# First sequence's triangular substitution issued on VectorE instead of GpSimd, in a four-stage transformer kernel

## The reference, cut to what matters

```python
att = jnp.where(tri, 0.0, -(kb @ jnp.swapaxes(k, -1, -2)))
for i in range(1, chunk):                      # chunk = 32
    upd = jnp.einsum('bhnj,bhnjk->bhnk', att[..., i, :], att)
    att = att.at[..., i, :i].add(upd[..., :i])
att = att + jnp.eye(chunk)
u = att @ v
w = att @ kb
```

## Time and profile before

| | us |
|---|---|
| three runs | 1975.06, 1981.21, 1982.22 |
| their median | 1981.21 |
| the profiled execution, device time | 1968.41 |
| its span, first to last instruction | 1966.6 |
| PE busy in the span | 1678.3 (85%) |
| DVE busy | 992.2 (50%) |
| POOL busy | 760.8 (39%) |
| ACT busy | 545.7 (28%) |

### The profile page before, as it was taken

One profiled execution on the slowest core, in us unless ns is written; L12 is line 12 of the kernel. 1 busy time (PEld: TensorE's weight loads), 2 busy tenths in 40 slices (PEclk: granted clock), 3 DMA queues, 4 the chain that ended last, 5 costly groups with the idle time before them and its releaser, 6 DMA issues. The chain is left out here.

```text
span 1966.6 us, 22843 instructions
## 1 busy us (share of the span) xinstructions
PE 1678.3 (85%) x8588; PEld 1121.4 (57%) x8588; DVE 992.2 (50%) x2206; ACT 545.7 (28%) x1180; POOL 760.8 (39%) x948
## 2 busy tenths in 40 slices
PE   4368898998999898896279999999967999999997
PEld 2245656666665666574236766666654555565564
DVE  3438798989898988784711111101113333444422
ACT  3242525253534435222221111111102222222121
POOL 1656667675757575812034423333221110111100
PEclk9679899898989999878589999999988999999999
DMA  3010111111111111101323322333120000000000
GB/s 106 17 22 17 23 49 23 44 27 28 44 28 44 28 34 28 33 12 32 129 86 86 86 47 56 81 79 82 22 50 4 3 20 22 22 22 22 11 0 22
DMA packets 108318, 77.99 MB, mean 40 GB/s; under 512 B 57384, under 2 KB 101424, under 8 KB 108208
## 3 DMA queue, kind: packets, MB, share of 16 engines
q1 hardware_dynamic: 95920, 59.74, 10.6%
q0 software_dynamic: 12288, 16.79, 4.9%
HBM read 51.34 MB, written 25.17 MB: 39 GB/s over the span
## 5 line engine op out<-in xcount | busy, mean ns | idle before, releaser
L383 DVE SCALAR_TENSOR_TENSOR a_firT<-a_v_ch,a_fir_lw,a_firT 128x511 f32<-128x511 f32 (+14 forms) x480 | 341.8, 777 | 0.0
L1530 DVE TENSOR_SCALAR ex_y<-ps,gT 128x256 f32<-128x256 f32 x64 | 31.0, 484 | 409.1 <-PE ps L1485 409.1
L1485 PE MATMUL ps<-ex_w,ex_hT 128*128 128x256 f32 x1024 | 223.5, 379 | 0.0
L1474 PE MATMUL ps<-ex_xT,ex_w 128*128 128x512 f32 x512 | 222.1, 594 | 0.0
L1440 POOL DMA_INDIRECT acc_dram<-ex_y,idxT x64 | 100.0, 1563 | 293.8 <-DVE ex_y L1530 293.8
L1485 PEld LDWEIGHTS ps<-ex_w,ex_hT 128*128 128x128 f32 x1024 | 194.0, 190 | 29.5 <-issue 3.8
L1512 ACT ACTIVATE ex_hT<-ps 128x512 f32<-128x512 f32 x128 | 76.6, 598 | 368.1 <-PE ps L1474 368.1
L1474 PEld LDWEIGHTS ps<-ex_xT,ex_w 128*128 128x128 f32 x512 | 97.7, 191 | 119.6 <-issue 119.2
L693 POOL TENSOR_TENSOR a_prod<-a_Yp,a_spare 128x126 f32<-128x126 f32 (+22 forms) x248 | 152.9, 616 | 26.4 <-DMA a_Yp<-y_dram 6.9
L1087 PE MATMUL ps<-a_firT,a_w_f 128*128 128x512 f32 x256 | 133.2, 645 | 18.7 <-DVE a_firT L383 18.7
L695 POOL TENSOR_TENSOR a_spare<-a_spare,a_prod 128x126 f32<-128x126 f32 (+22 forms) x248 | 133.0, 536 | 19.4
(11 more groups left out here) (275 smaller groups left out, 2947.1 us busy)
## 6 DMA issues: line engine op xcount, KB each, us to landing
ex_w<-in_L_ffn_w SPq DMA_DIRECT2D x16, 1024.0 KB, 8.6
a_xa<-in_L_attn_hidden_states SPq DMA_DIRECT2D x8, 512.0 KB, 4.0
a_xr<-in_L_attn_hidden_states SPq DMA_DIRECT2D x8, 512.0 KB, 4.6
a_Yp<-y_dram SPq DMA_DIRECT2D x16, 256.0 KB, 3.7
acc_dram<-a_xr SPq DMA_DIRECT2D x8, 512.0 KB, 4.3
xn_dram<-a_gxn SPq DMA_DIRECT2D x8, 512.0 KB, 3.2
l_xw<-acc_dram SPq DMA_DIRECT2D x8, 512.0 KB, 3.9
out<-l_xw SPq DMA_DIRECT2D x8, 512.0 KB, 2.9
```

What stands on the lines that cost most here:

```text
L383: nc.vector.scalar_tensor_tensor(out[:, kind, c, s:], v, w[:, c, n - 1 - s:n - s], out[:, kind, c, s:], ALU.mult, ALU.add).then_inc(fir_st ...
L1474: ins = nc.tensor.matmul(ps[:, n % 4, :], w1[j][:, c, f * P:(f + 1) * P], xT[j][:, c, half * 512:(half + 1) * 512], start=c == 0, stop=c = ...
L1485: ins = nc.tensor.matmul(dn_slot(n), hT[half][:, f, (n % 4) * CAP:(n % 4 + 1) * CAP], w2[j][:, f, :], start=f == 0, stop=f == FB - 1)
```

## The change

The substitution of sequence 0 is issued by DVE, between `norm_rows` of sequence 1 and the 20 early taps. POOL still clears and seeds `spare` for that sequence, and then goes straight on to `vk_of`. The other seven sequences stay on POOL. The products, the additions, their shapes and the semaphore counts are the same.

```diff
+            def solve_first():
+
+                dve.wait_ge(Yp_in, 32)
+                for k in range(31):
+                    c, r = k // 2 + 1, 31 - k
+                    m = prod[:, 0:c * r].rearrange("p (c i) -> p c i", c=c)
+                    dve.wait_ge(solved, 3 + 2 * k)
+                    nc.vector.tensor_tensor(m, spread(Yp[:, k + 1:32, k], 1, c), spread(Tp[:, 0:c, k], 2, r), ALU.mult).then_inc(solved, 1)
+                    dve.wait_ge(solved, 4 + 2 * k)
+                    nc.vector.tensor_tensor(Tp[:, 0:c, k + 1:32], Tp[:, 0:c, k + 1:32], m, ALU.add).then_inc(solved, 1)
+
             def join(b, d, e, r):
...
                 if nxt is not None:
                     norm_rows(nxt)
+                if b == 0:
+                    solve_first()
                 if d is not None:
                     scan(d, 3)
                 more(FIR_EARLY)
...
                 for half in range(2):
                     pool.memset(spare[64 * half:64 * half + 64, half:512:34], 1.0).then_inc(solved, 1)
+                if b == 0:
+                    pool.wait_ge(solved, n + 3)
+                    return
                 pool.wait_ge(Yp_in, b * 32 + 32)
```

## The result

The changed kernel takes 1956.39 us (median of four runs, 1951.79 to 1959.66) against 1978.35 us for the kernel before in the same comparison, a ratio of 0.9887 with a 95% interval of 0.9854 to 0.992. That is some 22 us less, with 16 to 29 us inside the interval. Run again with more repetitions the ratio is 0.9897 (0.9874 to 0.9921), or 20 us. The forecast was 19.1 us, 1962.1 us, within 1948 to 1972.

A forecast was written before the change was run, and what follows sets the result against it. POOL's 38.1 us substitution of sequence 0 was taken to hold up the first merge; on DVE it ends at 88.5 (69.52 + 17.7 + 1.3) instead of 107.61, 19.1 us off the 1981.21 us median: 1962.1 us, range 1948 to 1972.

The forecast's parts named there:

- The hole and what ends it: Before the first merge: PE, DVE and ACT empty from 83.8 to 107.6 us, ended by POOL's substitution, store and load.
- What is removed: On POOL: 62 substitution instructions leave, with 28.1 us after the first product and the stall; `vk` starts 41 us earlier.
- the 9.88 us: First product of POOL's substitution of sequence 0: its length, read as POOL kept from its operands by DVE's taps.
- that rival: At POOL's first `vk` product: the stall is POOL's own and moves there; gain 11.1 us, 1970.1 us, chance 0.06.
- The price on DVE: Substitution on DVE: 17.7 us for 62 instructions plus 1.3 us for meeting POOL's `vk`, ending at 88.5.
- POOL's `vk`: Beside the start of DVE's substitution: four of eight products each block a DVE instruction, up to 0.33 us, 1.3 us.
- Strided reads: Products reading a column of `Yp` on DVE: elements cost double, 2.9 us more; gain 16.2, 1965.0 us, chance 0.10.
- the row I judged it by: DVE instruction reading one element of four, 16 bytes apart: 0.17 us for 16 elements, as dense, so no penalty shows.
- the fit from two pairs: DVE instruction price from waiting pairs of 16 and 256 elements: 0.194 us fixed plus 1.0 ns per element.
- What moves: Taps and two key convolutions go behind the substitution; query convolution 1.2 us late, covered by 4.87 us DVE idle; SP order unchanged.
- The shift to the end: From first merge to kernel end: the 19.1 us should arrive whole; rival of losing it, about 1977 us, chance 0.05.
- The slower rival: Substitution slower on DVE than POOL, beyond 0.61 us per instruction; at 0.81, 50.2 us, time 1993.3 us, chance 0.05.

The follow-up runs named there:

- x11: Changed kernel with the second sequence's third to sixth projections and ACT's `tap3` on them moved ahead of the first merge; 0.9961 of the kernel before.
- x2: Kernel before, substitution still on POOL, with DVE's 20 early taps held until POOL's first substitution is done; 0.9953 of the kernel before.
- x1: The changed kernel run again without any edit; 1952.91 us against 1972.84 for the kernel before, 0.9897.
- x5: Changed kernel, each product of the first substitution preceded by one of the same shape reading a row of `Yp`, then overwritten; single time 1978.92 us.
- x6: Changed kernel with POOL's eight `vk` products held until the substitution is over; the substitution took 19.61 us against 20.23 in the changed kernel.
- x12: Changed kernel with POOL's eight `vk` products held until the substitution is over, timed; 1952.72 us, 0.9902 of the kernel before.
- x8: Changed kernel with each product of the first substitution issued four times, each waiting for the one before; 1.0083 of the kernel before.
- x4: Kernel before, with DVE's 20 early taps held until POOL's first product is done; 0.9978 of the kernel before.

## Why the prediction was right

**The hole and what ends it.** The reading of the waits held. One chain, substitution to store to load to merge, set the start of the merge and of what follows it: moving its end by -17.9, -9.3, -5.8, -3.4 and +14.7 us (table) moved the merge by as much, within 0.4 us, and the time by -20, -9, -3, -4 and +16 us, each within its interval of the move. These intervals reach 4 to 5 us to either side, so that the smaller moves are tested only roughly. x11 does not fit: its merge is 13.1 us earlier, its time only 7.7 us shorter (4 to 12).

**What is removed.** I read the 9.88 us as POOL kept waiting by the taps; x2, where the same product takes 0.25 us, shows it. In the changed kernel the first `vk` product takes 0.65 us, so the stall did not travel to it, and that rival falls.

**The price on DVE.** The sum was 17.7 us for 62 instructions and 1.3 us for POOL's `vk`, 19.0 in all; measured were 19.6 and 0.6, 20.2 in all, and in x1 19.6 and 1.0. Two terms were mis-sized, the instructions by 1.9 us too little and `vk` by 0.3 to 0.7 too much, and in part cancelled. Strided reads were a rival with a chance of 0.10 and a price of 2.9 us; in fact the products do cost more per element, 1.7 us in all by x5. The step that failed is the row I judged it by: 16 elements, where 0.6 ns each make 0.01 us, the last digit shown. The Trainium skill, page "SBUF — State Buffer", section "Door 1: The DMA port swizzle", has the penalty for each access to a new 16-byte line; x5 agrees for elements 128 bytes apart. The other 0.2 us are left to the fit from two pairs, which was not tested. For `vk` I counted four blocked instructions at 0.33 us; there were two, at some 0.3 us (0.48 and 0.54 against 0.19 and 0.20 in x6), and three in x1.

**What moves.** The query convolution was to be 1.2 us late and was 1.1, with the idle 4.87 us shrunk to 4.45. The SP order brought no surprise, with 7.56 us from the substitution's end to the merge (7.78 before).

**The shift to the end.** I let it reach the end whole. 18.1 us at the first merge were 15.1 at the last in that profile, and 17.6 became 16.5 in x1. The last merge, before and after:

```profile
827.48 3.40 PE L975 MATMUL ps<-a_TT,a_Y 32*32 32x32 f32 x64 [6.42 <-DMA a_TT<-t_dram]
...
812.34 3.40 PE L991 MATMUL ps<-a_TT,a_Y 32*32 32x32 f32 x64 [7.60 <-DMA a_TT<-t_dram]
```

In other profiles it changed more on the way: 9.3 to 2.9 in x2, 18.5 to 11.2 in x6 (in x12, the same kernel, 18.4 to 16.6), and 14.5 to 22.1 us late in x8. So a single profile shows the shift only to several us; the last section has what comes between. The profiled execution, forecast at 1949.3 us, took 1953.91, 14.5 us less than before and not 19.1. That the measured 22 and 20 us come so near the forecast of 19.1 is in part luck: both intervals hold anything from 16 to 25 us.

**The slower rival** needed 0.61 us per instruction; the pace was 20.23 / 62 = 0.33. x8, at 52.5 us for the substitution, shows that beyond its point of decision the loss is real: 16.4 us, where the rival's 50.2 us were to cost 12.1.

## What to carry to other kernels

In the fill of a pipeline a serial chain on a slow engine is priced at its full length, whatever the busy shares say; put it on a faster engine that is idle there and ahead of work that has slack, and check what the displaced work still meets. Before paying for another engine, look whether the chain is merely blocked: here half of the gain was order. And bringing work of a third engine forward into the hole can cost more than it fills, where the two engines block each other.

## What the runs showed of the hardware

**POOL and DVE hold each other up, as a rule by one instruction at a time.** In x11 DVE instructions of 0.3 to 0.4 us beside POOL's additions of 1.1 to 1.3 us last 1.0 to 1.4 us. The Trainium skill, page "SBUF — State Buffer", section "Who interferes with whom", says so for a DVE instruction with two SBUF inputs and a GpSimd one that reads SBUF, and these rows agree. Its wording, blocked until the other's instruction is done, does not cover the 9.88 us of the earlier trace rows, during which DVE went through some fifteen taps.

**A longer wait of PE goes with a lower clock behind it.** In the later sequences PE reaches the merge just about when `TT` lands. Where it waits 0.55 us (x1, fourth sequence) the clock granted in the next 11 us is 0.98 of full speed and the eight projection matmuls behind it take 3.70 us. The last row is of the busy time by stretch, with columns as in the earlier trace rows:

```profile
402.71 2.08 PE L991 MATMUL ps<-a_TT,a_Y 32*32 32x32 f32 x64 [0.55 <-DMA a_TT<-t_dram]
...
404.72 3.70 PE L972 MATMUL ps<-a_xT,a_w_qkv 128*128 128x512 f32 x8
...
402.70:413.70 11.00, 9.99 (x177) 7.42 (x178) 9.93 (x18) 7.26 (x13) 6.17 (x9) 0.98 0.15 46
```

In the same place of x5 it waits 2.32 us, the clock is 0.69, a mean between its two levels of 1.2 and 2.4 GHz, and the same eight take 6.52 us:

```profile
417.79 2.52 PE L994 MATMUL ps<-a_TT,a_Y 32*32 32x32 f32 x64 [2.32 <-DMA a_TT<-t_dram]
...
420.23 6.52 PE L975 MATMUL ps<-a_xT,a_w_qkv 128*128 128x512 f32 x8
...
417.80:428.80 11.00, 10.91 (x112) 6.64 (x112) 5.77 (x10) 3.87 (x7) 2.28 (x4) 0.69 0.12 41
```

In x5 the third to seventh sequences all wait so (2.3 to 2.7 us), and from merge to merge they take 105.5 to 105.8 us, where it is 102.2 to 102.8 in x1. In other profiles single sequences fall into it, as the sixth of the changed kernel (a wait of 1.60 us, then 104.3 us to the next merge, where its lead shrank from 17.2 to 15.2) and the fifth of x4. POOL's substitution lasts 41.0 us in these sequences of x1 and x5 alike. The slower rounds make up 14 of the 17 us that x5 loses between its first and last merge, and so most of its long time. In x6 and x12, one kernel, the last two rounds (103.9 and 104.0 us against 102.3 and 101.1) come to 4.5 us, and the spans differ by 3.9. That the wait brings the lower clock, and not one cause both, is argued and not shown, and the wait alone does not tell the round: 1.24 us in x2 were followed by 105.0 us, 1.27 in x6 by 102.7. What tips an execution from one rhythm to the other was not tried.
